# Query and key tiles turned by VectorE and DMA instead of TensorE, and the norm scale moved from the queries to the keys

## What is computed

```python
H, HKV, HD = (32, 8, 128)                        # G = 4 query heads for each key head
q = (x @ Wq.T).reshape(b, s, H, HD).transpose(0, 2, 1, 3)
k, v = ...                                       # the same with HKV heads
q = _rmsnorm(q, q_norm_w)
k = _rmsnorm(k, k_norm_w)
qg = q.reshape(b, HKV, G, s, HD)
scores = jnp.einsum('bkgqd,bksd->bkgqs', qg, k) / math.sqrt(HD)
bias = jnp.where(rel > 0, NEG_INF, slopes[:, :, None, None] * rel)
attn = jax.nn.softmax(scores + bias[None], axis=-1)
out = jnp.einsum('bkgqs,bksd->bkgqd', attn, v)
return out.transpose(0, 2, 1, 3).reshape(b, s, H * HD) @ Wo.T
```

## Time and profile before

| | |
|---|---|
| median of 3 runs | 1220.58 us (1220.3 to 1220.99) |
| span of the profiled execution | 1218.6 us |
| TensorE, matmul busy | 1206.2 us (99%) |
| VectorE busy | 834.9 us (69%) |
| ScalarE busy | 753.5 us (62%) |
| GpSimd busy | 652.8 us (54%) |
| granted TensorE clock | 1.000 |
| SyncE's DMA queue | 92.29 MB, 22.2% of 16 engines |

### The profile page before, as it was taken

One profiled execution on the slowest core, in us unless ns is written; L12 is line 12 of the kernel. 1 busy time (PEld: TensorE's weight loads), 2 busy tenths in 40 slices (PEclk: granted clock), 3 DMA queues, 4 the chain that ended last, 5 costly groups with the idle time before them and its releaser, 6 DMA issues.

```text
span 1218.6 us, 18533 instructions
## 1 busy us (share of the span) xinstructions
PE 1206.2 (99%) x6368; PEld 1062.1 (87%) x6368; DVE 834.9 (69%) x2035; ACT 753.5 (62%) x1758; POOL 652.8 (54%) x526
## 2 busy tenths in 40 slices
PE   6999999999999999999999999999999999999999
PEld 5888888899998999999999999999999888888887
DVE  7876665776666577677677677667767878755555
ACT  4554442357677767767768767767767774544442
POOL 5796561635675625724824824823824343865550
DMA  6152222212213123122122122122122020221101
GB/s 235 42 175 94 103 105 104 94 47 87 79 44 104 44 79 103 39 84 96 44 87 89 50 87 87 53 79 96 53 78 87 20 68 9 71 69 53 52 18 69
DMA packets 33596, 93.77 MB, mean 77 GB/s; under 512 B 4128, under 2 KB 5056, under 8 KB 31456
## 3 DMA queue, kind: packets, MB, share of 16 engines
q1 hardware_dynamic: 33264, 92.29, 22.2%
q10 hardware_dynamic: 240, 0.30, 0.1%
HBM read 62.69 MB, written 29.88 MB: 76 GB/s over the span
## 4 chain that ended last, share of the span: by engine, by line
PE 98%; DVE 1%; DMA 0%; ACT 0%; SPq 0%; issue 0%
PE bank L369 22%; PE bank L367 22%; PE bank L368 21%; PE bank L674 6%; PE bank L479 4%; PE bank L473 4%; PE bank L474 4%; PE bank L688 3%; PE bank L693 3%; PE bank L689 3%; PE bank L619 2%; PE bank L395 1%; PE bank L655 1%; PE bank L622 1%; PE bank L383 1%; DMA x_rows<-x 0%
## 5 line engine op out<-in xcount | busy, mean ns | idle before, releaser
L1066 ACT ACTIVATE prob<-prob,neg_top 128x128 f32<-128x128 f32 (+3 forms) x256 | 141.2, 554 | 87.6 <-DVE neg_top L1517 56.9
L1817 POOL TENSOR_TENSOR rows<-rows,row_root_y 128x640 f32<-128x640 f32 x64 | 80.5, 1257 | 194.1 <-DVE row_root_y L1205 192.9
L1811 POOL TENSOR_TENSOR square<-rows 128x640 f32<-128x640 f32 x64 | 79.3, 1254 | 158.7 <-DVE rows L1560 131.1
L1686 POOL TENSOR_TENSOR w_l_late<-raw_late,w_h_late 128x512 fp32r<-128x512 f32 (+1 forms) x59 | 91.5, 1565 | 71.8 <-ACT w_h_late L809 71.8
L1075 ACT ACTIVATE prob<-prob,inverse 128x128 f32<-128x128 f32 (+3 forms) x252 | 121.1, 553 | 4.4 <-DVE inverse L1522 4.4
L1535 DVE TENSOR_TENSOR probT_l<-bank,probT_h 128x512 fp32r<-128x512 f32 x160 | 101.4, 683 | 28.5 <-ACT probT_h L1081 28.5
L1081 ACT CAST probT_h<-bank 128x512 fp32r<-128x512 f32 x160 | 84.6, 596 | 41.4 <-PE bank L674 41.4
L1281 DVE SCALAR_TENSOR_TENSOR x_rows<-bank,x_rows 128x512 f32<-128x512 f32 x111 | 74.8, 687 | 44.4 <-PE bank L479 44.4
L367 PE MATMUL bank<-o_h,oT_h 128*128 128x512 f32 x256 | 104.7, 409 | 0.0
L369 PE MATMUL bank<-o_h,oT_l 128*128 128x512 f32 x256 | 100.8, 394 | 0.0
L368 PE MATMUL bank<-o_l,oT_h 128*128 128x512 f32 x256 | 99.8, 390 | 0.0
(11 more groups left out here) (237 smaller groups left out, 3808.5 us busy)
## 6 DMA issues: line engine op xcount, KB each, us to landing
x_ring<-x_between SPq DMA_DIRECT2D x64, 256.0 KB, 2.6
x_between<-x_ring SPq DMA_DIRECT2D x56, 256.0 KB, 2.0
raw_late<-w_qkv SPq DMA_DIRECT2D x8, 1536.0 KB, 6.5
raw_early<-ffn_w SPq DMA_DIRECT2D x21, 512.0 KB, 4.1
scaled<-raw_early SPq DMA_DIRECT2D x21, 512.0 KB, 2.7
raw_late<-scaled SPq DMA_DIRECT2D x21, 512.0 KB, 3.7
raw_late<-w_o SPq DMA_DIRECT2D x8, 1024.0 KB, 5.0
x_between<-x_rows SPq DMA_DIRECT2D x8, 256.0 KB, 2.0
```

The lines of the kernel that those rows point to most:

```text
L1066: last = act.activation(p, p, ACT.Exp, bias=neg_top[:, h:h + 1], scale=-1.0, accum_out=total[:, h:h + 1])
L1686: return pool.tensor_tensor(lo, raw, hi.bitcast(F32), ALU.subtract)
```

## The change

It holds for the units 3 to 61 (`BLOCKED`, 59 of them). At the end of its slot n VectorE turns the normed rows of unit n + 2 (four query heads and the key head, 128 tokens x 640) within squares of 32x32, into row_blocks. SyncE stores this to DRAM, waits for it, and loads it back in four DMAs with the squares in their places, which gives the fully turned tiles in turned_rows, the squares in another order. ScalarE and VectorE make the rounded parts and rests from there instead of from two PSUM banks; TensorE turns these units' rows no more, and its scores(n) wait for q_rest_done and k_rest_done. The scale moves from the queries (512 columns) to the keys (128 columns), in all units. The scratch space for DMA descriptors is halved. The code of the units 0 to 2, 62 and 63 is otherwise as before.

```diff
 SHARED = UNITS - 3, UNITS - 1
+
+SQ = 32
+BLOCKED = range(3, UNITS - 2)
...
+        row_blocks = sb("row_blocks", [P // SQ, G + 1, SQ])
+        turned_rows = sb("turned_rows", [P // SQ, G + 1, SQ])
...
+        def by_block(queries):
+
+            return queries[:, :, :].rearrange("p h (a t) -> p a h t", t=SQ)
+
+        def blocked_nth(n):
+
+            return BLOCKED.index(n)
...
                 if keys_first(n):
                     scores_by_parts(n)
                     return
-                pe.wait_ge(evac[turned_q.bank], turned_q.nth)
-                pe.wait_ge(evac[turned_k.bank], turned_k.nth)
+                if n in BLOCKED:
+                    pe.wait_ge(q_rest_done, blocked_nth(n) + 1)
+                    pe.wait_ge(k_rest_done, blocked_nth(n) + 1)
+                else:
+                    turned_q, turned_k = results["turn_q", n], results["turn_k", n]
+                    pe.wait_ge(evac[turned_q.bank], turned_q.nth)
+                    pe.wait_ge(evac[turned_k.bank], turned_k.nth)
...
-                    if n + 1 < UNITS:
+                    if n + 1 < UNITS and n + 1 not in BLOCKED:
                         turn_rows(n + 1)
...
-                turn_rows(n + 1)
+                if n + 1 not in BLOCKED:
+                    turn_rows(n + 1)
...
             def turn_rows(n):
                 g, _, t = unit(n)
                 if n % (B * TB) == 0:
-                    act.wait_ge(q_scale_done, 1 + g + 1)
+                    act.wait_ge(k_scale_done, 1 + g + 1)
+                if n in BLOCKED:
+
+                    act.wait_ge(rows_back, 16 * (P // SQ) * (blocked_nth(n) + 1))
+                    act.copy(by_block(qT_h), turned_rows[:, :, 0:G, :]).then_inc(qT_hi_done, 1)
+                    act.activation(kT_h[:, t * P:(t + 1) * P].rearrange("p (a q) -> p a q", q=SQ), turned_rows[:, :, G, :], ACT.Copy,
+                                   scale=k_scale[:, g:g + 1]).then_inc(kT_hi_done, 1)
+                    return
                 if keys_first(n):
                     turn_keys(n)
                 r = results["turn_q", n]
                 act.wait_ge(full[r.bank], r.nth)
-                act.activation(qT_h[:, :, :], banks[r.bank][:, :].rearrange("p (h q) -> p h q", h=G), ACT.Copy,
-                               scale=q_scale[:, g:g + 1]).then_inc(qT_hi_done, 1)
+                act.copy(qT_h[:, :, :], banks[r.bank][:, :].rearrange("p (h q) -> p h q", h=G)).then_inc(qT_hi_done, 1)
                 if not keys_first(n):
                     turn_keys(n)
 
             def turn_keys(n):
-                t = unit(n)[2]
+                g, _, t = unit(n)
                 r = results["turn_k", n]
                 act.wait_ge(full[r.bank], r.nth)
-                act.copy(kT_h[:, t * P:(t + 1) * P], banks[r.bank][:, 0:P]).then_inc(kT_hi_done, 1)
+                act.activation(kT_h[:, t * P:(t + 1) * P], banks[r.bank][:, 0:P], ACT.Copy, scale=k_scale[:, g:g + 1]).then_inc(kT_hi_done, 1)
...
             def turn_rows(n):
                 g, _, t = unit(n)
+                if n in BLOCKED:
+                    dve.wait_ge(qT_hi_done, n + 1)
+                    dve.tensor_tensor(by_block(qT_l), turned_rows[:, :, 0:G, :], by_block(qT_h).bitcast(F32), ALU.subtract).then_inc(q_rest_done, 1)
+                    cols = slice(t * P, (t + 1) * P)
+                    dve.wait_ge(kT_hi_done, n + 1)
+                    dve.scalar_tensor_tensor(kT_l[:, cols].rearrange("p (a q) -> p a q", q=SQ), turned_rows[:, :, G, :], k_scale[:, g:g + 1],
+                                             kT_h[:, cols].bitcast(F32).rearrange("p (a q) -> p a q", q=SQ),
+                                             ALU.mult, ALU.subtract).then_inc(k_rest_done, 1)
+                    return
                 if keys_first(n):
                     turn_keys(n)
                 r = results["turn_q", n]
                 dve.wait_ge(qT_hi_done, n + 1)
-                dve.scalar_tensor_tensor(qT_l[:, :, :], banks[r.bank][:, :].rearrange("p (h q) -> p h q", h=G), q_scale[:, g:g + 1],
-                                         qT_h[:, :, :].bitcast(F32), ALU.mult, ALU.subtract).then_inc(evac[r.bank], 1)
+                dve.tensor_tensor(qT_l[:, :, :], banks[r.bank][:, :].rearrange("p (h q) -> p h q", h=G), qT_h[:, :, :].bitcast(F32),
+                                  ALU.subtract).then_inc(evac[r.bank], 1)
                 if not keys_first(n):
                     turn_keys(n)
 
             def turn_keys(n):
-                t = unit(n)[2]
+                g, _, t = unit(n)
                 r = results["turn_k", n]
                 cols = slice(t * P, (t + 1) * P)
                 dve.wait_ge(kT_hi_done, n + 1)
-                dve.tensor_tensor(kT_l[:, cols], banks[r.bank][:, 0:P], kT_h[:, cols].bitcast(F32), ALU.subtract).then_inc(evac[r.bank], 1)
+                dve.scalar_tensor_tensor(kT_l[:, cols], banks[r.bank][:, 0:P], k_scale[:, g:g + 1], kT_h[:, cols].bitcast(F32),
+                                         ALU.mult, ALU.subtract).then_inc(evac[r.bank], 1)
+
+            def block_rows(n):
+
+                dve.wait_ge(rows_normed, n + 1)
+                if blocked_nth(n):
+                    dve.wait_ge(rows_away, 16 * blocked_nth(n))
+                dve.transpose(row_blocks[:, :, :, :], rows[:, n % LEAD, 0:G + 1, :].rearrange("p h (b k) -> p b h k", k=SQ)).then_inc(rows_blocked, 1)
...
                 if n:
                     turn_probabilities(n)
+                if n + 2 in BLOCKED:
+                    block_rows(n + 2)
...
+            def send_rows(n):
+
+                nth = blocked_nth(n)
+                away = row_turns[nth % 2]
+                sp.wait_ge(rows_blocked, nth + 1)
+                if nth > 1:
+                    sp.wait_ge(rows_back, 16 * (P // SQ) * (nth - 1))
+                sp.dma_start(away, row_blocks[:, :, :, :].rearrange("p b h t -> p (b h t)")).then_inc(rows_away, 16)
+                if nth:
+                    sp.wait_ge(q_rest_done, nth)
+                    sp.wait_ge(k_rest_done, nth)
+                sp.wait_ge(rows_away, 16 * (nth + 1))
+                for b in range(P // SQ):
+                    sp.dma_start(turned_rows[b * SQ:(b + 1) * SQ, :, :, :].rearrange("k a h t -> k a (h t)"),
+                                 away.rearrange("(a k) (b c) -> b k a c", k=SQ, b=P // SQ)[b]).then_inc(rows_back, 16)
...
             for n in range(UNITS):
                 g, at = divmod(n, B * TB)
+                if n + 1 in BLOCKED:
+                    send_rows(n + 1)
                 if at == 1:
                     if g < HKV - 1:
                         load_qkv(g + 1)
...
+    row_turns = nc.dram_tensor("row_turns", (2, P, (G + 1) * P), F32, kind="Internal").ap()
```

More of the change, by code:

```diff
@@ L84, with build @@
 Result = namedtuple("Result", "bank nth")
-def build(nc, scaled, x_between, x, ffn_w, ffn_fac, ffn_fix, factor_lo, w_qkv, w_o, norm_w, out):
+def build(nc, scaled, x_between, row_turns, x, ffn_w, ffn_fac, ffn_fix, factor_lo, w_qkv, w_o, norm_w, out):
     pe, act, dve, pool, sp = nc.tensor, nc.scalar, nc.vector, nc.gpsimd, nc.sync
@@ L122, in build @@
             semaphore(n) for n in ("whole_pair_done", "token_sums_done", "token_sums_lo", "qkv_mixed", "v_lo_done"))
-        squares_done, rows_normed, bias_done, q_scale_done, ident_done, zeroed = (
-            semaphore(n) for n in ("squares_done", "rows_normed", "bias_done", "q_scale_done", "ident_done", "zeroed"))
+        squares_done, rows_normed, bias_done, k_scale_done, ident_done, zeroed = (
+            semaphore(n) for n in ("squares_done", "rows_normed", "bias_done", "k_scale_done", "ident_done", "zeroed"))
         weights_mixed, whole_done = semaphore("weights_mixed"), semaphore("whole_done")
+        rows_blocked, rows_away, rows_back, q_rest_done, k_rest_done = (
+            semaphore(n) for n in ("rows_blocked", "rows_away", "rows_back", "q_rest_done", "k_rest_done"))
         mix_done, mix_hi_done, mix_lo_done, silu_done, product_done = (
@@ L152, in build @@
         ident = sb("ident", [P])
-        norm_ws, w_product, q_scale = sb("norm_ws", [2]), sb("w_product", [1]), sb("q_scale", [HKV])
+        norm_ws, w_product, k_scale = sb("norm_ws", [2]), sb("w_product", [1]), sb("k_scale", [HKV])
         stats, mv = sb("stats", [B * TB, 6]), sb("mv", [B * TB, 2])
@@ L641, in scores @@
                 keys = (unit(n)[2] + 1) * P
-                turned_q, turned_k = results["turn_q", n], results["turn_k", n]
                 if keys_first(n):
@@ L1450, in from_ffn_to_attention @@
                 turn_normed(1, 1, (2, 3))
-                dve.wait_ge(q_scale_done, 1 + HKV)
+                dve.wait_ge(k_scale_done, 1 + HKV)
                 dve.wait_ge(bias_done, 1 + 2 * G)
@@ L1914, in pool_program @@
             pool.wait_ge(norm_in, 16)
-            pool.tensor_tensor(w_product[:, :], norm_ws[:, 0:1], norm_ws[:, 1:2], ALU.mult).then_inc(q_scale_done, 1)
-            pool.wait_ge(q_scale_done, 1)
```

(11 more changed lines are left out.)

## The result

The changed kernel takes 1306.0 us (1305.6 to 1308.9) against 1220.4 for the kernel before beside it: 1.070 times as long, 95% interval 1.069 to 1.072. The forecast, 1246.4 with a range of 1228 to 1279, had the direction and missed the size: 85 us were lost where 26 had been worked out. The profiled execution has a span of 1304.3 us.

The account below looks back on a forecast made before the run. TensorE's queue was taken to bound the kernel, with VectorE's chain to oT_l close behind. Transpose less removed turns gave +16.6 us, late rows 9.2: +25.8 on 1220.6, so 1246.4 us, range 1228 to 1279.

Parts of the forecast that it names:

- what bounds: TensorE's queue bounds the kernel; from slot 12 on, VectorE's chain to oT_l is only 0.15 to 0.55 us ahead of need.
- the 0.15 that the sum hands on from tile 2: VectorE ends tile 2's slot 0.76 us later, TensorE's slot grows 0.61; the next slot gets 0.15, 1.8 us in all.
- the transpose: VectorE's 128x640 transpose ahead of the next scores takes 0.76 us, bounds 0.4 and 1.4, and delays everything to oT_l.
- the sum without its trip: Effects of removed turns and added transpose over all slots, before any lateness of the rows' DRAM transfers: +16.6 us.
- the removed turns: TensorE's five turns cost 0.54 us a slot, 31.9 us over 59 slots if nothing else were late.
- Rival (1): VectorE takes the first scores on time despite the transpose; 21.8 us won at no delay, 1198.8 us; chance 10%.
- the sources are SBUF: nothing or 0.1 us: Rests and rounded parts read SBUF instead of PSUM, with the scale moved to keys: nothing or 0.1 us, off the bound.
- the trip: Rows' way to DRAM and back takes 5.3 us, bounds 4.8 and 7.0; hidden except in two slots of eight, 9.2 us.
- Rival (3): The DRAM round trip is the bound, from about 6.3 us on; TensorE waits at scores; 27 us more, 1273; chance 13%.
- slot 60, "I count as 0.3 longer": Slot 60, differently ordered from the slots before it, was counted as 0.3 us longer.
- the slots with at = 4 and at = 2, 4.2 and 5.0 us: Rows come late with weight splits queued behind on ScalarE: 0.7 us six times, 4.2, and about 1.0 five times, 5.0.
- the slack of 1.38 us in four slots: Time by which oT_l precedes project_out's first matmul, summed over tiles 0 to 3: 0.18, 0.50, 0.15 and 0.55 us.

Follow-up runs that it names:

- I: Changed kernel without VectorE's transpose and the rows' way through DRAM, heads made straight from the normed rows; 1220.7 us, 1.000.
- B: Changed kernel without the rows' store and loads through DRAM; ScalarE and VectorE take the rows from row_blocks in SBUF; 1254.4 us, 1.028.
- D: Changed kernel with SyncE's ring load issued behind the rows' store instead of ahead of it, nothing left out; 1270.7 us, 1.042.
- A: Kernel before with only VectorE's transpose of unit n + 2 added at the end of slot n, into a tile nobody reads; 1243.6 us, 1.019.
- F: Kernel before with VectorE's rests of the turned rows made from an SBUF tile of zeros instead of PSUM; 1236.8 us, 1.014.
- J: Changed kernel without transpose and way through DRAM, and with GpSimd's squares and norms replaced by fills that only write; 1206.1 us, 0.988.
- E: Changed kernel with GpSimd's squares and norms of the attention rows replaced by fills that only write; 1283.9 us, 1.052.
- H: Changed kernel with the ring load behind the rows' store and VectorE's transpose ahead of the turned probabilities, nothing left out; 1247.2 us, 1.023.

## Why the prediction was right and wrong

**The account.** Going from one kernel to the next in the medians: turns removed, no hold, 1206.1 - 1220.6 = -14.5; the hold +14.6 (I); the transpose +33.7 (B); the trip with the ring load behind it +16.3 (D); the ring load ahead of it +35.3 (after). The sum is +85.4. The forecast, +25.8, failed at two steps above all: it took the rests from SBUF for free, and it priced the trip as if SyncE's queue were empty. Its steps against this:

- **Right: what bounds.** TensorE's order bounds the kernel before, and the chain from the scores to oT_l is nearly as long. A's slots are the forecast's to 0.02 us but for tile 3 (14.43; the list has 14.3, but leaves out the 0.15 that the sum hands on from tile 2), and in the kernel after TensorE waits for oT_l 48 times, once for each slot from 12 to 59.
- **Right: the transpose.** 0.76 us from start to start was taken from a subtraction and a reduction; it is 0.76. B less what the hold costs by F (16.6) is 1237.8, and the sum without its trip was 1220.6 + 16.6 = 1237.2.
- **A little high: the removed turns.** Rival (1) had 21.8 for a head that isn't moved; J has 14.5, since slots 12 to 59 win 0.76 in four and not 1.37. Slots 2 to 11 do win theirs in J (5.7 for 5.4).
- **Wrong: "the sources are SBUF: nothing or 0.1 us".** It is 14.6 to 16.6 us (I - J and F), and up to 22.1 in the changed kernel (after - E), where the key rests stand in SyncE's loop of slots 2 to 11. The row that could have told me is GpSimd's timeline beside VectorE's rests; I looked at the rests' own durations alone. The Trainium skill's rule named at F stood there to be read.
- **Wrong in size: the trip, 9.2 for 51.6.** Its parts were near: out 2.2 to 2.3 (2.1), back 3.4 (3.2). The step that failed is the one that adds 5.3 us to the end of VectorE's tail. It priced the transfer from when the rows are turned and left SyncE's own queue out: the rows' store stands behind ring_store, a wait for it to land, and ring_load. This costs up to 0.84 us of late issue in slot 25 and 1.2 of slower landing. Worse, it closes a loop through VectorE's sum: once around takes 11.6 us in slot 25, whatever TensorE has to do. In slots 2 to 11, which were to win, D takes 13 of the lost 21 us away (and so does E: the ring load and the held key rests lengthen the same loop). Rival (3) had part of the mechanism ("TensorE waits at scores", decided from 6.3 us on; measured 6.9), with 13% and 27 us; it counted tiles 0 and 1 and the two slots behind weights, and no loop. TensorE's wait for oT_l stayed the larger one, 49.1 us for 30.5 at the scores.
- **Wrong: slot 60, "I count as 0.3 longer".** It is 4.7 longer. B has 6.84 there, so 3.9 of it are the trip, which has no cover in a slot of 6 us.
- **Near: the slots with at = 4 and at = 2, 4.2 and 5.0 us.** Both terms make the next slot late. For at = 4, D is the case: ScalarE waits 0.84 us for the rows in slot 28, with three weight splits behind, and the next slots (at = 5, from slot 21 on) have 11.35 us where those with at = 1 have 10.58; B has 10.54. That is 0.8 us, against 0.7 in the forecast. For the w_qkv load it is the changed kernel: its five slots with at = 3 are together 7.7 us longer than with at = 7 (1.7 of this is the lower clock of slot 27, 17.43 x 0.10), against 5.0; in D, where the rows' store doesn't wait for the ring store to land, the two are alike (14.49 and 14.50). So the 9.2 wasn't wrong, but most of the trip was missing from it.

D is 16.3 above B, 17.7 by the spans (1270.0 and 1252.3): 5.8 in slots 2 to 11, 5.1 in slots 12 to 55, nearly all of it in the slots with at = 5, 5.6 in slots 60 and 61, and 1.2 ahead of the first scores, where other kernels of this case are up to 2 us apart as well.

What remains open: the steps don't simply add, and another order of them would share the loss differently. The transpose costs 23 us alone (A) and 33.7 in the ladder. The forecast's own terms have a reason that fits, which no run takes apart: A still finds the slack of 1.38 us in four slots, and in the ladder the removed turns have spent it. In slots 2 to 11 D and E give back 13 us each of the 19 that lie between B and the changed kernel, so of the ladder's 35.3 for the ring load a part could as well be put down to the hold. No kernel that does the whole change is faster than the kernel before: the best is H, 1247.2.

## What to carry to other kernels

Price a transfer from the moment at which its queue is free to issue it, and write down what stands ahead of it there, waits for landings included: the order of two issues was worth 35.3 us here, and the turns that were moved 31.9 at most. When an operand moves from PSUM to SBUF, look at what GpSimd does at that time before calling it free. And work removed from the busiest engine is worth the slack of the next late input (14.5 us of 32 here), which others may spend.

## What the runs showed of the hardware

- A 128x640 fp32 transpose in 32x32 squares on VectorE: 0.83 us record, 0.76 from start to start; one of 32 columns 0.20.
- A 320 KB store to DRAM lands in 2.2 to 2.3 us in most slots, with a 256 KB load issued well ahead of it (2.9 us in slot 24 of the kernel after) or 0.4 us behind it (slot 25 of D), and in 3.2 to 3.6 with that load 0.4 to 0.5 us ahead. Four 80 KB loads back take 1.74 us to issue and 3.4 until their reader starts.
- A rest of 128x512 with both sources in SBUF takes 0.69 us, or 1.50 in the slots where GpSimd's norm is reading SBUF; beside a GpSimd fill it takes 0.68. A rest of 128x128 takes 0.34, or 1.40 beside GpSimd's squares.
- The granted clock was 1.00 in every window of the kernel before that is shown. In the kernel after it falls four times, at 296.9, 392.5, 624.6 (in slot 27) and 1051.3. TensorE's timeline, with its idle time ahead of slot 3, the windows of slots 3 and 4, and the window of the first fall:

```profile
297.84 0.77 PE L384 MATMUL bank<-kT,qT_h 128*128 128x512 f32 x1 [3.91 <-issue]
```

```profile
297.84:314.07 16.23, 16.23 (x73) 14.14 (x74) 9.62 (x22) 11.77 (x27) 8.38 (x6) 0.82 0.25 73
314.07:326.34 12.27, 11.32 (x63) 10.04 (x62) 10.51 (x32) 6.63 (x22) 4.38 (x4) 1.00 0.31 98
296.90:303.70 6.80, 5.86 (x14) 4.68 (x15) 6.36 (x14) 4.44 (x10) 5.55 (x4) 0.50 0.39 122
```

The clock fell 0.9 us before the end of 3.91 us of idle time and stood at the lower of its levels, 1.2 and not 2.4 GHz, for 6.8 us; the slot's mean is 0.82. The work that this leaves undone is 16.23 x 0.18 = 2.9 us in this slot. The mean of the span is 0.993, some 8.5 us, against 0.997 in D and 1.000 in B. A part of what the account puts down to the trip is therefore the clock; the records don't show how much of it would have been idle time anyway.
